# A graph network's first pass: register loads cut smaller and moved, and a shorter lead for the gathers at the start of each pass

## The reference

```python
def _L0_gnn_ref(embedding, edge_index, W1, b1, We1, be1, Wn1, bn1, We2, be2, W2, b2):
    src, dst = (edge_index[0], edge_index[1])
    h = _gcn_conv(embedding, src, dst, ones_e, W1, b1, n)       # sums of x[src] per dst, scaled by degrees, @ W1
    h = h / jnp.maximum(jnp.sqrt(jnp.sum(h * h, axis=-1, keepdims=True)), 1e-12)
    ev = _edge_encoder(h, src, dst, We1, be1)                    # sigmoid(h[src] @ .. + h[dst] @ .. + be)
    na = _node_encoder(h, src, dst, ev, Wn1, bn1, n)             # relu(segment_sum(ev * h[src], dst) @ Wn + bn)
    ev2 = _edge_encoder(na, src, dst, We2, be2)
    g = _node_encoder(na, src, dst, ev2, Wn1, bn1, n)
    return _gcn_conv(g, src, dst, ev2, W2, b2, n)
h = jnp.maximum(_layernorm(x, axis=-1), 0.0)
x = x + _L0_gnn_ref(h, edge_index, ...)
```

## Time and profile before

| | |
|---|---|
| median of three runs | 3305.12 us (3301.57 to 3305.61) |
| the profiled execution | 3307.64 us, span 3305.8 us |
| granted TensorE clock, mean | 0.929 of 2.4 GHz |
| busy share of the span | PE 79%, PEld 69%, DVE 64%, ACT 49%, POOL 56% |
| first pass | from about 130 us to 960 us |
| half passes 1, 2, 3 | 1048 to 1710 us, 1810 to 2568 us, 2625 to 3281 us |

### The profile page before, as it was taken

How to read it: one execution, slowest core, us unless ns; L and a number is a source line. 1 busy time by engine, 2 the same in 40 slices (tenths; PEclk the granted TensorE clock), 3 DMA queues, 4 the chain that set the end, 5 groups by cost and what they waited for, 6 DMA issues and landing times.

```text
span 3305.8 us, 59188 instructions
## 1 busy us (share of the span) xinstructions
PE 2621.3 (79%) x16470; PEld 2268.9 (69%) x16470; DVE 2107.4 (64%) x6199; ACT 1624.3 (49%) x3249; POOL 1854.2 (56%) x1816
## 2 busy tenths in 40 slices
PE   0677768888896777777789999999999767777675
PEld 0344447888894666667688788888888666666665
DVE  4677776555625666666674566666666457666667
ACT  7266656666666555555554344444444422323332
POOL 5345555555305677767710666666661267777773
PEclk9789889999998899998999999999999888988998
DMA  4244445555542333333322444444442433333333
GB/s 115 83 149 175 165 165 196 192 194 200 194 159 83 101 104 112 101 115 101 101 78 78 137 134 126 130 135 137 135 135 82 143 99 98 115 101 100 115 100 95
DMA packets 185597, 419.60 MB, mean 127 GB/s; under 512 B 36655, under 2 KB 136700, under 8 KB 175533
## 3 DMA queue, kind: packets, MB, share of 16 engines
q10 hardware_dynamic: 83703, 244.23, 20.8%
q0 software_dynamic: 61472, 140.49, 14.7%
q1 hardware_dynamic: 40118, 31.23, 3.0%
HBM read 311.35 MB, written 102.16 MB: 125 GB/s over the span
## 4 chain that ended last, share of the span: by engine, by line
PE 68%; issue 12%; DVE 10%; another core or an unknown queue 3%; ACT 2%; ACTq 1%; DMA 1%; DVEq 1%; SPq 1%; POOL 0%; POOLq 0%
PE ps L1137 18%; PE ps_high L1129 16%; PE ps_high L1137 12%; PE ps L1070 7%; PE ps L1054 3%; PE ps_high L1087 3%; PE ps_high L1082 2%; DVE tab_area L1541 2%; DVE acc L1612 1%; PE ps_high L1216 1%; ACT tab_area L776 1%; DVE xbuf L1527 1%; PE ps L1249 1%; DVE weights L1588 1%
## 5 line engine op out<-in xcount | busy, mean ns | idle before, releaser
L601 POOL DMA_INDIRECT rows<-table,edge_src x1664 | 1748.2, 1051 | 1135.0 <-SPq L496 603.3
L1129 PE MATMUL ps_high<-rows,weights 128*128 x2784 | 644.4, 341 | 379.6 <-issue 199.7
L1137 PE MATMUL ps<-tab_area,acc 128*128 128x129 f32 (+2 forms) x4410 | 816.1, 324 | 7.7 <-issue 7.2
L1129 PEld LDWEIGHTS ps_high<-rows,weights 128*128 128x128 f32 x2784 | 471.0, 202 | 480.1 <-issue 258.7
L1137 PEld LDWEIGHTS ps<-tab_area,acc 128*128 128x128 f32 x4410 | 691.3, 204 | 52.3 <-issue 8.5
L876 ACT ACTIVATE step<-xbuf,rows 128x128 f32 x928 | 357.8, 394 | 673.3 <-PE ps_high L1129 451.1
L1612 DVE TENSOR_TENSOR acc<-acc 128x640 f32<-128x640 f32 x735 | 604.1, 822 | 104.3 <-ACT acc L885 70.1
L1137 PE MATMUL ps_high<-tab_area,acc 128*128 128x129 f32 (+2 forms) x2940 | 584.7, 324 | 0.4 <-issue 0.4
L1595 DVE TENSOR_TENSOR acc<-acc,ps_high 128x129 f32 (+1 forms) x948 | 334.3, 353 | 369.7 <-PE ps_high L1129 265.3
L776 ACT ACTIVATE tab_area<-ps_high x816 | 403.5, 494 | 253.6 <-PE ps_high L1087 188.0
L1137 PEld LDWEIGHTS ps_high<-tab_area,acc 128*128 128x128 f32 x2940 | 475.1, 204 | 28.6 <-DVE acc L1595 0.8
(11 more groups left out here) (242 smaller groups left out, 2168.5 us busy)
## 6 DMA issues: line engine op xcount, KB each, us to landing
acc<-counts ACTq DMA_DIRECT2D x105, 1120.0 KB
counts<-tab_area ACTq DMA_DIRECT2D x51, 1568.0 KB
acc<-counts ACTq DMA_DIRECT2D x25, 1568.0 KB
rows<-table,edge_src POOLq DMA_INDIRECT x1664
table<-tab_area SPq DMA_DIRECT2D x6, 903.0 KB, 4.6
table<-acc SPq DMA_DIRECT2D x7, 448.0 KB, 4.1
table<-tab_area SPq DMA_DIRECT2D x6, 455.0 KB, 3.7
table<-tab_area SPq DMA_DIRECT2D x6, 448.0 KB, 3.0
```

The costliest lines, as they stand in the source:

```text
L601: nc.gpsimd.indirect_dma_start(rows[:, t % UNROLL, 0:row_floats[k]], None, tables[k], bass.IndirectOffsetOnAxis(ap=edge_src[:, t:t + 1], a ...
L1129: nc.tensor.matmul(ps[DENSE_BANKS + m % PAIR_BANKS][:, 0:WIDTH[k]], weights[:, m % W_RING, :], rows[:, bass.ds(known["slots"][m % UNROLL], ...
L1137: ins = nc.tensor.matmul(ps[j][:, 0:WIDTH[k]], gate_blocks[:, n % S_RING, j * PART:(j + 1) * PART], table[:, h, 0:WIDTH[k]], start=(h == 0 ...
```

## The change

There are three parts. Only the first pass and the gathers are touched.

- **TensorE's numbers.** Places in the ring come eight at a time, behind the third pair (`u == 2`) of the eight before; the needs of these eight, two numbers that stand four apart, come behind the sixth (`u == 5`). Those of the first eight pairs are loaded ahead of slot 0. So 29 times 16 and four numbers become 58 times eight and two.
- **VectorE's numbers.** Four at a time, behind `weigh`, for the four pairs after the next; 29 loads become 116.
- **The gathers.** Gather `t` may be `min(16, 8 + t // 4)` ahead, where it was 16, in each of the four passes. The first to wait is the 11th (`t = 10`), and from `t = 32` on the waits are as before.

```diff
+FIRST_AHEAD = 8
@@ gather_pass
-                    if t >= UNROLL:
-
-                        pool.wait_ge(slots_free, tiles_before(k) + t - UNROLL + LAG + 1)
+                    ahead = min(UNROLL, FIRST_AHEAD + t // 4)
+                    if t >= ahead:
+
+                        pool.wait_ge(slots_free, tiles_before(k) + t - ahead + LAG + 1)
@@ helpers
-        def load_last(engine, part, i, top):
+        def quad_loader(engine, *parts):
+
+            loaded = []
+
+            def load(end):
+                while len(loaded) * QUAD < min(end, HALF_PAIRS):
+                    at = slice(len(loaded) * QUAD, (len(loaded) + 1) * QUAD)
+                    loaded.append([nc.values_load_multi_w_load_instructions(
+                        pair_row[0:1, part, at], engines=[engine], min_val=0, max_val=top,
...
+            def number(m, part=0):
+                return loaded[m // QUAD][part][m % QUAD]
+
+            return load, number
+
+        def load_eight(engine, part, i, top, step=1):
 
             return nc.values_load_multi_w_load_instructions(
-                pair_row[0:1, part, i * UNROLL + QUAD - 1:(i + 1) * UNROLL:QUAD], engines=[engine], min_val=0, max_val=top,
+                pair_row[0:1, part, i * 2 * QUAD + step - 1:(i + 1) * 2 * QUAD:step], engines=[engine], min_val=0, max_val=top,
@@ first_pass on TensorE: multiply
-                    u, q = m % UNROLL, m // QUAD
+                    u, q, turn = m % (2 * QUAD), m // QUAD, m // (2 * QUAD)
                     if u == 0:
-                        first_pass.slots = load_pairs(TEN, 0, 1, m // UNROLL, UNROLL - 1)
-                        first_pass.needs = load_last(TEN, 2, m // UNROLL, HALF)
+                        first_pass.slots, first_pass.needs = first_pass.slots_next, first_pass.needs_next
                     if m % QUAD == 0:
                         pe.wait_ge(weights_ready, q + 1)
-                        pe.wait_ge(tiles_landed[0], first_pass.needs[q % (UNROLL // QUAD)])
+                        pe.wait_ge(tiles_landed[0], first_pass.needs[q % 2])
...
+                    if u == 2 and m + 2 * QUAD < HALF_PAIRS:
+                        first_pass.slots_next = load_eight(TEN, 1, turn + 1, UNROLL - 1)
+                    if u == 5 and m + 2 * QUAD < HALF_PAIRS:
+                        first_pass.needs_next = load_eight(TEN, 2, turn + 1, HALF, QUAD)
@@ ahead of slot 0
+                first_pass.slots_next, first_pass.needs_next = load_eight(TEN, 1, 0, UNROLL - 1), load_eight(TEN, 2, 0, HALF, QUAD)
@@ first_pass on VectorE: add_pair
-                    if m % UNROLL == 0:
-                        first_pass.nodes = load_pairs(VEC, 0, 0, m // UNROLL, SPARE)
                     if m % QUAD == 0 and m // QUAD + 1 < PAIR_QUADS:
                         weigh(m // QUAD + 1)
+                        load_nodes(m + 2 * QUAD)
                     v.wait_ge(pairs_done[0], m + 2)
-                    add(first_pass.nodes[m % UNROLL], ps[m % FIRST_BANKS][:, 0:FEAT])
+                    add(node_of(m), ps[m % FIRST_BANKS][:, 0:FEAT])
```

More of the change, by code:

```diff
@@ L367, in load_pairs @@
                 skip_runtime_bounds_check_because="the staircase has no more node tiles, slots and edge tiles")[1]
-        def load_last(engine, part, i, top):
+        def quad_loader(engine, *parts):
[5 more added lines that the diff above has]
+                        pair_row[0:1, part, at], engines=[engine], min_val=0, max_val=top,
+                        skip_runtime_bounds_check_because="the staircase has no more node tiles, slots and edge tiles")[1] for part, top in parts])
+            def number(m, part=0):
+                return loaded[m // QUAD][part][m % QUAD]
+            return load, number
+        def load_eight(engine, part, i, top, step=1):
             return nc.values_load_multi_w_load_instructions(
-                pair_row[0:1, part, i * UNROLL + QUAD - 1:(i + 1) * UNROLL:QUAD], engines=[engine], min_val=0, max_val=top,
+                pair_row[0:1, part, i * 2 * QUAD + step - 1:(i + 1) * 2 * QUAD:step], engines=[engine], min_val=0, max_val=top,
                 skip_runtime_bounds_check_because="the staircase has no more edge tiles")[1]
@@ L1544, in add_pair @@
                 def add_pair(m):
[L1545 to L1546 removed]
                     if m % QUAD == 0 and m // QUAD + 1 < PAIR_QUADS:
                         weigh(m // QUAD + 1)
+                        load_nodes(m + 2 * QUAD)
                     v.wait_ge(pairs_done[0], m + 2)
[L1550 removed]
+                    add(node_of(m), ps[m % FIRST_BANKS][:, 0:FEAT])
                 low = load_half(VEC, 2, LOW_TILES)
                 first_pass.sums = 0
+                load_nodes, node_of = quad_loader(VEC, (0, SPARE))
                 weigh(0)
+                load_nodes(QUAD)
                 for b in range(LM_RING - 1):
```

## The result

The changed kernel takes 3283.19 us (median of four runs, 3278.75 to 3286.01) where the one before takes 3305.36 us on the same chip. The ratio is 0.9929, 95% interval 0.9914 to 0.9945: 22 us or 0.7% less, where 62 less were forecast. Its profiled execution has a span of 3276.9 us, 28.9 less than that of before: it is the fastest of its four, and the one of before lies 2.5 us above its median. What follows is read from these two traces.

A forecast was written before the change was run, and what follows sets the result against it. It took TensorE as the bound from 500 to 960 us and no engine from 155 to 500. Early −22, late −30, VectorE's loads 0 and gathers −10 made −62 us against 3307.6: 3243 us by the median, range 3205 to 3290.

The forecast's parts named there:

- The late stage, −30: First pass, 500 to 960 us: smaller TensorE loads and a higher clock save 30 us, with ends of 0 and −45.
- the loads that meet heavy DMA traffic and grow to 2.1 us can stick out again: +4: First pass, 500 to 960 us: TensorE loads lengthened by DMA traffic cost 4 us.
- the clock term, −8: First pass, 500 to 960 us: fewer stalls at TensorE's loads raise its granted clock from 0.97, saving 8 us.
- The early stage, −22: First pass, 155 to 500 us: TensorE's changed loads save 22 us, with ends of −4 and −45.
- −17 − 4 + 3: First pass, 155 to 500 us: twelve load blocks give back 17 us idle time and 4 us clock; new loads cost 3.
- The rival that this stage doesn't follow TensorE: First pass, 155 to 500 us: ScalarE or VectorE is the bound, only −4 of −22 is left, 3261 us; chance 0.15.
- VectorE's loads, 0: First pass: 116 loads of 0.31 us replace 29 of 1.10 us, hidden by VectorE's idle time, for 0 us.
- Gathers, −10: Starts of the passes: ten unguarded gathers in place of 16 shorten the halts and save 10 us, between −43 and +15.
- the rival in which the halts go: Pass starts: the run of gathers causes the halts, which go almost entirely, −43 not −10, 3210 us; chance 0.16.
- The 6 us of the half passes: Starts of the half passes: halts summing to 35 us shrink by 6 us with the new gather lead.
- the weakest step: Pass starts: late semaphores that halt the other engines come with POOL's dense run of gathers; no row names the cause.
- The lead did not starve the pairs: Rival, passes 1 and 3: the shorter gather lead leaves pairs without tiles, +15 in place of −10, 3268 us; chance 0.14.

The follow-up runs named there:

- e6: The changed kernel with 16-bit tables of needs and entries, its stores of counts cut from 1568 KB to 32 KB each: 3201.57 us.
- e7: The kernel before the change, with 16-bit tables of needs and entries and its stores of counts cut from 1568 KB to 32 KB each: 3237.86 us.
- the base: The kernel before the change with its tables of needs and entries as 16-bit instead of 32-bit numbers: 3192.94 us on one quick chip, 3190.42 us on another.

## Why the prediction was wrong, step by step

**The late stage, −30: the step that failed.** Measured 6.5 us. The mis-sized term is the one in its sentence "the loads that meet heavy DMA traffic and grow to 2.1 us can stick out again: +4". I took the maxima of the earlier trace rows for rare events spread over all loads. They are a fixed quarter of the late loads (45 of 168), tied to the store of every 16th slot. `count` had 20 of them before; what is new is 24 of the pairs', 20 of which start within 1 us behind a long one of `count`, such as 1.8 + 2.0 us against the cover of 1.7 us that the prediction itself had worked out. What the term measured: moving the loads away from the store wins 24.7 us in this half on late chip E, the kind of chip that was predicted for, and 44 to 47 on quick chips. With 24.7 in place of 4 the prediction's own sum is −26 − 8 + 24.7 = −9, near the measured −6.5 (an estimate, as those kernels have the 16-bit tables and `count`'s old long loads are moved with the others). The idle time at pairs did fall by 25 us (31.6 to 6.1, forecast 26), and 20 came back ahead of the pieces, 14.6 of it as issue. With it the clock term, −8, mostly went: 0.96 to 0.98, 2.4 us of busy time. That the store is what stretches the loads is shown (e6: none long without it), and that their place costs this half its time is shown on quick chips B and D and on late chip E; on late chip C, without such a control, less is seen. The forecast would have been too high even without that. With no store in either kernel the change is worth 17.8 us on a quick chip; part of the time at the old loads was itself stretched (six of the late L371 took 2.6 to 3.7 us).

**The early stage, −22.** Slots 32 to 416 hold the first block and ten of the other twelve, and took 14.0 us less. The first block gave 4.6, forecast 4. The ten gave 9.4, where −17 − 4 + 3 for twelve is −15 for ten (an estimate). So this stage too is short by some 6 us, though within its bounds; as in the late stage, part came back behind the new loads, 14.5 us of issue ahead of L1103, where +3 was charged. Here 32 of the 140 loads are long. The rival that this stage doesn't follow TensorE, which left it 4 us, is out: ScalarE's wait for counts fell from 94.4 to 77.5 us. On quick chips the same edit gave 21 to 27 us, and the clock went from 0.90 to 0.99 (chip A), on the first chip to 0.95. The difference, 7 to 13 us, goes with the kind of chip; what in it keeps the time back was not separated.

**VectorE's loads, 0.** Right, as far as quick chips show: putting them back changes nothing. This row has 115 of them, 344 ns in the median:

```profile
L377 DVEq TENSOR_LOAD <-pair_row x115: 338/344/1096, 161.5 to 902.5; - x115
```

The floor of about 600 ns for a tensor_load in the Trainium skill ("DMA: Bandwidth & Descriptors", "Latency and other measured facts") does not hold for these 116 loads.

**Gathers, −10.** In pass 0 more went than the 4 us forecast: slots 0 to 32 are 7.8 us shorter, the two halts of the earlier trace rows (8 us) are gone, and POOL has stopped by then. In the seven late-chip traces with the shorter lead these slots take 20.6 to 21.5 us, against 29.3 in the only one with the longer lead, that of before; on quick chips they take 18 to 20 us with either (e6 and e7, which fill the table in these slots, aside). That fits the rival in which the halts go, in this pass alone, but is not shown: the loads ahead of slot 0 came with the shorter lead, and one trace stands for before. The 6 us of the half passes came to nothing: 2.7 and 3.0 us were won between the first and last pair of passes 1 and 2, and 2.4 lost in pass 3. On quick chips there is no halt from an unknown source in any pass, with either lead. So the weakest step, that the dense run of gathers makes the halts, does not hold by itself: the same run is there without halts. Whether the lead matters on a late chip was not run with a base beside it and stays open. The lead did not starve the pairs: no pass became longer by more than 2.4 us.

**The tells.** Issue ahead of L1071: 14.5 and 6.1 us, forecast under 12 and 8. Clock 0.94 and 0.98, forecast over 0.95 and 0.98. The last count came 28.4 us sooner, forecast 56. The one to look for was named under "wrong would be": idle time of the same size behind the third and sixth pairs. It stands ahead of L1091 (issue 2.1 us before, 16.7 after) and, in the early stage, ahead of L1103 (20.9 us).

## What to carry to other kernels

A load or wait whose median is short and whose maximum is four times that is to be split by what else runs then, before its cost is taken from the median: here the phase in a period of 16 slots decides it. A small load on the sequencer that also issues the matmuls is free only while the queued work outlasts it; put it where nothing large is being stored. Two in a row there look like the costly case, though no run tells that apart. When idle time falls at one line, add up all lines of that engine before calling it won.

## What the runs showed of the hardware

- **Loads of 16-bit numbers are slow.** SyncE's load of 16 entries takes 972 ns in the median as 32-bit numbers and 3254 as 16-bit ones; ScalarE's 16 needs 3380 ns against about 1020 for 16 numbers of 32 bits; the two strided needs take the same in either form (527 ns in the median as 16-bit numbers, 529 at the least as 32-bit ones). The two rows are before's and the base's:

```profile
L487 SPq TENSOR_LOAD <-entry_row x104: 967/972/4072, 136.1 to 3234.7; - x104
```

```profile
L492 SPq TENSOR_LOAD <-entry_row x104: 3248/3254/7010, 135.7 to 3118.5; - x104
```

  That is the likely cost of the base, which was not separated further.
- **A store of 1568 KB from SBUF stretches the register loads that follow its issue.** In the changed kernel all 42 late loads of TensorE that start 1 to 5 us behind it take 1.2 to 2.5 us in place of 0.53 or 0.59, 3 of the 7 that start within 1 us do, and none of those later than 5 us is over 0.8. In the other kernels with such loads the last long one starts 5.3 us behind.
- **Chips differ by 5.6%** for one kernel (3155 to 3333 us), and the slower ones are those whose traces have semaphores that come late.
